# Transposes in place of two POOL reductions, and the feed-forward weights made ready inside the scan stage

## The reference

```python
x = x + _L0_attn_ref(_layernorm(x), context, Wq, Wk, Wv, Wout, bout)
...
x = x + _L1_attn_ref(_layernorm(x), A, W_b, b_b, W_c, b_c, D, W_t, b_t, W_o, b_o)   # decay scan over 64 steps
x = x + _L1_ffn_ref(_layernorm(x), W_fc, b_fc, A_fc, B_fc, W_proj, b_proj, A_proj, B_proj)

def fake_quant_weight(w):
    scale = jnp.max(jnp.abs(w)) / 127
    wq = jnp.clip(jnp.round(w / scale), -128, 127) * scale
    return w + jax.lax.stop_gradient(wq - w)

def qat_lora_linear(x, W, b, A, B):
    return x @ fake_quant_weight(W).T + b + 2.0 * ((x @ A.T) @ B.T)
```

## Time and profile before

| what | us |
|---|---|
| median of 3 runs (lowest, highest) | 3278.88 (3271.15, 3282.62) |
| time of the profiled execution | 3276.0 |
| its span, first to last instruction | 3274.2 |
| TensorE busy | 3023.0 (92% of the span) |
| VectorE, ScalarE, POOL busy | 2199.9, 2009.3, 926.0 |
| mean granted TensorE clock | 0.963 |
| wide prologue: first load issued, first score product | 658.4, 721.1 |
| scan stage: first load issued, last vector pass ends | 2914.6, 3025.0 |
| feed-forward stage: first load issued, `fc` of block 0, `project` of block 0 | 3029.4, 3063.1, 3094.2 |

### The profile page before, as it was taken

How to read it: one execution, slowest core, us unless ns; L and a number is a source line. 1 busy time by engine, 2 the same in 40 slices (tenths; PEclk the granted TensorE clock), 3 DMA queues, 4 the chain that set the end, 5 groups by cost and what they waited for, 6 DMA issues and landing times. The chain is left out here.

```text
span 3274.2 us, 88570 instructions
## 1 busy us (share of the span) xinstructions
PE 3023.0 (92%) x34175; PEld 2461.8 (75%) x34175; DVE 2199.9 (67%) x5201; ACT 2009.3 (61%) x3697; POOL 926.0 (28%) x800
## 2 busy tenths in 40 slices
PE   8999999959999999999977999999999997878699
PEld 6888888737877877877866887787787786544598
DVE  5777777756666666666634778778778776664643
ACT  5777777647767667767733666666666675332353
POOL 3444444336555555655620000000000000110110
PEclk9999999969999999999988999999999999889699
DMA  2112111148887888887973111111111110741200
GB/s 79 58 59 66 62 58 58 38 104 151 150 136 145 150 136 148 152 146 140 173 197 119 34 41 53 47 41 47 54 41 47 47 34 24 230 141 52 88 20 26
DMA packets 664877, 294.34 MB, mean 90 GB/s; under 512 B 550747, under 2 KB 639792, under 8 KB 664576
## 3 DMA queue, kind: packets, MB, share of 16 engines
q1 hardware_dynamic: 626176, 237.71, 34.1%
q10 hardware_dynamic: 38400, 52.44, 4.8%
HBM read 125.95 MB, written 29.88 MB: 48 GB/s over the span
## 5 line engine op out<-in xcount | busy, mean ns | idle before, releaser
L1096 POOL TENSOR_TENSOR wide_parts<-wide_prob,wide_parts 128x1024 f16<-128x1024 f32 x256 | 548.7, 2143 | 398.1 <-ACT wide_parts L1282 329.9
L1385 DVE TENSOR_REDUCE wide_row_max<-wide_score 128x1 f32<-128x1024 f32 x256 | 312.7, 1221 | 163.2 <-PE wide_score L1130 161.6
L1130 PE MATMUL wide_score<-wide_kT,wide_qT 128*128 128x512 f32 x1536 | 413.1, 404 | 7.1 <-ACT wide_prob L1270 5.5
L1270 ACT ACTIVATE wide_prob<-wide_score,wide_neg_max 128x1024 f32<-128x1024 f32 x256 | 285.2, 1114 | 163.7 <-DVE wide_neg_max L1388 158.2
L641 ACT ACTIVATE mask_prob<-mask_prob,mask_row_min 128x256 f32<-128x256 f32 x512 | 232.1, 503 | 161.6 <-DVE mask_row_min L730 161.6
L1130 PEld LDWEIGHTS wide_score<-wide_kT,wide_qT 128*128 128x128 f32 x1536 | 277.1, 189 | 67.9 <-issue 8.9
L1282 ACT ACTIVATE wide_parts<-wide_prob 128x1024 f16<-128x1024 f32 x256 | 269.9, 1054 | 18.5 <-ACT wide_prob L1270 9.2
L2217 DVE TENSOR_REDUCE cell_row_max<-cell_score 128x8 f32<-128x512 f32 x192 | 131.2, 684 | 171.6 <-PE cell_score L1853 169.8
L1146 PE MATMUL wide_turn<-wide_probT,wide_v 128*128 128x256 f16 x1536 | 189.6, 273 | 2.8 <-DMA wide_probT<-wide_parts 2.8
L1146 PE MATMUL wide_pv<-wide_probT,wide_v 128*128 128x256 f16 x1536 | 190.3, 274 | 1.2 <-DMA wide_probT<-wide_parts 1.2
L111 POOL TENSOR_TENSOR cell_var_eps<-cell_mean_var,const_eps 128x4 f32<-128x4 f32 x8 | 1.6, 200 | 670.5 <-DVE cell_mean_var L105 670.5
(11 more groups left out here) (338 smaller groups left out, 6878.3 us busy)
## 6 DMA issues: line engine op xcount, KB each, us to landing
cell_w_stage<-cell_weights ACTq DMA_DIRECT2D x24, 768.0 KB, 6.0
mask_ctx<-in_ctx SPq DMA_DIRECT2D x32, 512.0 KB, 3.9
ctx_ctx<-in_ctx SPq DMA_DIRECT2D x32, 512.0 KB, 4.4
...
wide_probT<-wide_parts SPq DMA_TRANSPOSE x512, 3.3
...
```

The lines of the kernel that those rows point to most:

```text
L1096: pool.tensor_tensor(parts[:, s % 2, LO, :], prob[:, s % 2, :], parts[:, s % 2, HI, :], ALU.subtract).then_inc(part_lo, 1)
L1130: mm = pe.matmul(score[:, s % 2, half * 512:(half + 1) * 512], qT[:, u_par, a, s * P:(s + 1) * P], kT[:, par, b, half * 512:(half + 1) * 5 ...
L1270: act.activation(prob[:, s % 2, :], score[:, s % 2, :], ACT.Exp, bias=neg_max[:, s % 2:s % 2 + 1], scale=SHARP, accum_out=row_sum[:, u_par ...
L1385: dve.tensor_reduce(row_max[:, one], score[:, s % 2, :], AX.X, ALU.max).then_inc(max_found, 1)
```

## The change

Three things. In the wide prologue the two reductions on POOL give way to two small transposes on TensorE with a row maximum and a spreading copy on VectorE between them; all `rstd_of` of POOL then stand in a row ahead of its bias additions, and the load of the whole W_v is issued one place earlier, ahead of block 1. The preparation of the feed-forward weights moves into a class `FfnWeights`, whose loads stand at the end of the scan stage's load queue and whose passes are placed in the scan's steps 1 to 7; its maxima go by transposes too, its low parts are subtracted on POOL, and it uses three PSUM banks (3, 6, 7) by turns. And x stays in SBUF from the scan to the feed-forward stage: the scan no longer stores it and the last stage no longer loads it. The scan's steps are written out instead of looped.

```diff
+    def vector_max(self, dve, m):
+        name = self.NAMES[m]
+        dve.wait_ge(self.w_loaded[name], 16)
+        dve.tensor_reduce(self.amax[:, m:m + 1], self.flat(self.w[name]), AX.X, ALU.max, apply_absolute_value=True).then_inc(self.max_found, 1)
+    def tensor_max_rows(self, pe, bank):
+        pe.wait_ge(self.max_found, 2)
+        pe.transpose(bank[0:2, 0:P], self.amax[:, :], self.ident[:, :]).then_inc(self.max_turned, 1)
+    def vector_spread_max(self, dve, bank):
+        dve.wait_ge(self.max_turned, 1)
+        dve.tensor_reduce(self.all_max[:, :], bank[0:2, 0:P], AX.X, ALU.max).then_inc(self.max_spread, 1)
+        dve.wait_ge(self.max_spread, 1)
+        dve.tensor_scalar(self.max_row[:, :], self.all_max[:, :].to_broadcast([2, P]), 1.0, None, ALU.mult).then_inc(self.max_spread, 1)
+    def tensor_share_max(self, pe, bank):
+        pe.wait_ge(self.max_spread, 2)
+        pe.transpose(bank[:, P:P + 2], self.max_row[:, :], self.ident[0:2, 0:2]).then_inc(self.max_shared, 1)
+    def vector_quantise(self, dve, bank, m):
+        one, steps = slice(m, m + 1), m * 4 + 1
+        src, q = self.flat(self.w[self.NAMES[m]]), self.flat(self.wq[self.NAMES[m]])
+        if m == 0:
+            dve.wait_ge(self.max_shared, 1)
...
+            dve.tensor_scalar(self.scale[:, :], bank[:, P:P + 2], 1.0 / self.QMAX, None, ALU.mult).then_inc(self.quant_step, 1)
+        dve.wait_ge(self.quant_step, 1)
+        dve.reciprocal(self.inv_scale[:, one], self.scale[:, one]).then_inc(self.quant_step, 1)
+        dve.wait_ge(self.quant_step, steps + 1)
+        dve.tensor_scalar(q, src, self.inv_scale[:, one], self.MAGIC, ALU.mult, ALU.add).then_inc(self.quant_step, 1)
...
+        dve.tensor_scalar(q, q, self.QMAX, self.scale[:, one], ALU.min, ALU.mult).then_inc(self.quant_step, 1)
...
+        dve.tensor_tensor(q, q, src, ALU.subtract).then_inc(self.rest_found, 1)
+        dve.wait_ge(self.rest_found, m + 1)
+        dve.tensor_tensor(q, src, q, ALU.add).then_inc(self.quant_done, 1)
...
+    def bank_of(self, pe, banks, kind, n):
+        i = self.uses.index((kind, n))
+        if i >= 3:
+            before, m = self.uses[i - 3]
+            pe.wait_ge(self.prep_copied if before == "turn" else self.weights_ready, m + 1)
+        return banks[i % 3]
+    def tensor_turn(self, pe, banks, first, end):
+        if first == 0:
+            pe.wait_ge(self.small_loaded, self.SMALL_LOADED)
+        elif first == self.small_turns:
+            pe.wait_ge(self.quant_done, 1)
+        elif first == self.fc_turns:
+            pe.wait_ge(self.quant_done, 2)
+        for n in range(first, end):
+            dst, parts = self.turns[n]
+            bank = self.bank_of(pe, banks, "turn", n)
+            at = 0
+            for src, width in parts:
+                k = src.shape[0]
+                mm = pe.transpose(bank[0:src.shape[1], at:at + k], src, self.ident[0:k, 0:k])
+                at += k
+            mm.then_inc(self.prep_turned, 1)
+    def scalar_copy(self, act, banks, first, end):
+        for n in range(first, end):
+            dst = self.turns[n][0]
+            bank = banks[self.uses.index(("turn", n)) % 3]
+            act.wait_ge(self.prep_turned, n + 1)
+            act.activation(dst, bank[0:dst.shape[0], 0:dst.shape[1]], ACT.Copy).then_inc(self.prep_copied, 1)
+    def tensor_low_rank(self, pe, banks, first, end):
+        pe.wait_ge(self.prep_copied, self.fc_turns if first < self.fc_loras else len(self.turns))
+        for n in range(first, end):
+            out, lhsT, rhs, _ = self.products[n]
+            bank = self.bank_of(pe, banks, "lora", n)
+            pe.matmul(bank[:, 0:rhs.shape[1]], lhsT, rhs, start=True, stop=True).then_inc(self.lora_ready, 1)
+    def vector_merge(self, dve, banks, first, end):
+        for n in range(first, end):
+            out = self.products[n][0]
+            bank = banks[self.uses.index(("lora", n)) % 3]
+            dve.wait_ge(self.lora_ready, n + 1)
+            dve.scalar_tensor_tensor(out, bank[:, 0:out.shape[1]], self.LORA, out, ALU.mult, ALU.add).then_inc(self.weights_ready, 1)
+    def scalar_hi(self, act, first, end):
+        for n in range(first, end):
+            out, _, _, split = self.products[n]
+            act.wait_ge(self.weights_ready, n + 1)
+            act.activation(split[self.HI], out, ACT.Copy).then_inc(self.w_hi, 1)
+    def gpsimd_lo(self, pool, first, end):
+        for n in range(first, end):
+            out, _, _, split = self.products[n]
+            pool.wait_ge(self.w_hi, n + 1)
+            pool.tensor_tensor(split[self.LO], out, split[self.HI].bitcast(F32), ALU.subtract).then_inc(self.w_lo, 1)
...
+            if n == 1:
+                sp.dma_start(w_v_all, W_v.rearrange("(t p) i -> p t i", p=CP)).then_inc(w_v_loaded, 16)
             sp.dma_start(x_all[:, n * SUB:(n + 1) * SUB, :], block_rows(x_in[n * BLK:(n + 1) * BLK, :])).then_inc(x_loaded[n], 16)
             if n == 0:
                 weights(0, 0)
                 sp.dma_start(out_bias[:, :], b_out.partition_broadcast(P)).then_inc(bias_loaded, 16)
-            if n == 1:
-                sp.dma_start(w_v_all, W_v.rearrange("(t p) i -> p t i", p=CP)).then_inc(w_v_loaded, 16)
         weights(0, 1)
...
-        for n in range(2):
-            rstd_of(n)
-        for m in range(2):
-            pool.wait_ge(top_found, m + 1)
-            pool.partition_all_reduce(all_top[:, m:m + 1], top[:, m:m + 1], P, RMAX).then_inc(top_shared, 1)
-        for n in range(2, NBLK - 1):
+        for n in range(NBLK):
             rstd_of(n)
         pool.wait_ge(bias_loaded, 16)
-        add_bias(0)
-        rstd_of(NBLK - 1)
-        for n in range(1, POOL_BIASES):
+        for n in range(POOL_BIASES):
...
+            if n == 1:
+                pe.wait_ge(top_found, 2)
+                pe.transpose(misc_ps[0:2, 0:P], top[:, :], ident[:, :]).then_inc(top_turned, 1)
+                pe.wait_ge(top_spread, 2)
+                pe.transpose(misc_ps[:, P:P + 2], top_row[:, :], ident[0:2, 0:2]).then_inc(top_shared, 1)
...
+        def spread_top():
+            dve.wait_ge(top_turned, 1)
+            dve.tensor_reduce(all_top[:, :], misc_ps[0:2, 0:P], AX.X, ALU.max).then_inc(top_spread, 1)
+            dve.wait_ge(top_spread, 1)
+            dve.tensor_scalar(top_row[:, :], all_top[:, :].to_broadcast([2, P]), 1.0, None, ALU.mult).then_inc(top_spread, 1)
         def scale_values():
-            dve.wait_ge(top_shared, 2)
-            dve.tensor_tensor(bound[:, :], all_top[:, 0:1], all_top[:, 1:2], ALU.mult).then_inc(v_scaled, 1)
+            dve.wait_ge(top_shared, 1)
+            dve.tensor_scalar(bound[:, :], misc_ps[:, P:P + 1], CD / V_TOP, None, ALU.mult).then_inc(v_scaled, 1)
             dve.wait_ge(v_scaled, 1)
-            dve.tensor_scalar(v_up[:, :], bound[:, :], CD / V_TOP, 1e-30, ALU.mult, ALU.max).then_inc(v_scaled, 1)
+            dve.tensor_scalar(v_up[:, :], misc_ps[:, P + 1:P + 2], bound[:, :], 1e-30, ALU.mult, ALU.max).then_inc(v_scaled, 1)
             dve.wait_ge(v_scaled, 2)
             dve.reciprocal(v_down[:, :], v_up[:, :]).then_inc(v_scaled, 1)
...
         find_top(1, w_v_all)
+        spread_top()
         stats_of(2)
         scale_values()
...
-    turn_banks, in_banks, out_banks, prep_banks = bank[0:2], bank[2:4], bank[4:6], bank[6:8]
+    turn_banks, in_banks, out_banks, prep_banks = bank[0:2], bank[2:3], bank[4:6], bank[6:8]
+    ffn_banks = [bank[3], bank[6], bank[7]]
...
-        step(0, 0, True)
-        with eng.Fori(0, (NBLK - 4) // 2) as i:
-            for k in (1, 2):
-                step(i * 2 + k, k % 2, False)
-        for n in range(NBLK - 3, NBLK):
-            step(n, n % 2, False)
+        for n in range(NBLK):
+            step(n, n % 2, n == 0)
...
+        ffn.load(sp)
...
-        with pool.Fori(0, NBLK) as n:
+        for n in range(8):
             norm.gpsimd_rstd(pool, n)
+        ffn.gpsimd_lo(pool, 0, ffn.loras)
...
+            if n == 7:
+                ffn.tensor_turn(pe, ffn_banks, ffn.fc_turns, len(ffn.turns))
...
+            if n == 3:
+                ffn.tensor_share_max(pe, ffn_banks[2])
...
+            if n == 2:
+                ffn.tensor_max_rows(pe, ffn_banks[2])
+            if n == 4:
+                pe.wait_ge(ffn.quant_step, 1)
+                ffn.tensor_turn(pe, ffn_banks, 0, ffn.small_turns)
+            if n == 5:
+                ffn.tensor_turn(pe, ffn_banks, ffn.small_turns, ffn.fc_turns)
+            if n == 6:
+                ffn.tensor_low_rank(pe, ffn_banks, 0, ffn.fc_loras)
...
+        ffn.tensor_low_rank(pe, ffn_banks, ffn.fc_loras, ffn.loras)
...
-        def store(n):
-            act.wait_ge(y_ready, (n + 1) * 2)
-            act.dma_start(block_rows(x_out[rows(n * BLK, BLK), :]), of_block(n)).then_inc(y_stored, 16)
...
-            store(n)
+            if n == 4:
+                ffn.scalar_copy(act, ffn_banks, 0, ffn.small_turns)
+            if n == 5:
```

(53 more changed lines are left out.)

281 lines of the change are left out of this document (105 added, 176 removed).

## The result

| | before | after |
|---|---|---|
| median of 4 runs each on one chip, us | 3275.92 | 3246.22 |
| lowest, highest | 3271.15, 3282.62 | 3242.45, 3248.70 |
| time and span of the profiled execution | 3276.0, 3274.2 | 3242.45, 3240.5 |

The ratio is 0.9907 (95% interval 0.9885 to 0.9929): 29.7 us faster by the medians, 33.6 by the profiled executions (the profiled execution of the changed kernel was the fastest of its four). I had said 3245, a gain of 32.4.

A forecast was written before the change was run, and what follows sets the result against it. TensorE's own work was taken to bound the kernel, except at stage starts, where chains between engines do. 9.5 + 23.9 - 1.0 = 32.4 us of gain, forecast as 3245 us, range 3235 to 3258.

The forecast's parts named there:

- Wide prologue, 9.5 us: Start of wide attention: replacing POOL's reductions and their pauses by small transposes brings block 3's normalising 9.5 us earlier.
- no POOL pause over 1 us: Wide prologue: expected sign in the profile that POOL no longer pauses longer than 1 us.
- Scan, 18.2 us later: Scan stage: preparing the feed-forward weights there makes its last work end at 3043.2 instead of 3025.0, 18.2 us later.
- My three additions, 0.4, 2.0 and 2.4 us: Scan steps 2 and 3 together, 4, and 5: TensorE time added by weight transposes, delaying block 6's output by 4.9 us.
- Between the stages, 27.1 us: From the scan's end to block 0's second product in the last stage: 27.1 us, with all weights ready.
- The tail's sum, 23.9 us: Scan's end and last stage: the old 69.2 us less 18.2 and 27.1 leaves a gain of 23.9 us.
- One more clearing, 1.0 us: End of the program: one further clearing costs 1.0 us, taken off the gain.
- 2: Wide prologue: POOL's pauses are not the reductions', so that part gains nothing; 3255 us, chance 0.06.
- 3: Scan step 4 through block 0's first product: clock stays low, costing 47 us; 3292 us, slower, chance 0.03.
- Rival 1: Scan's last steps: TensorE's clock falls, costing 12 to 18 us; 3257 us, chance 0.10.
- The prediction's own sign of being wrong, a clock near 0.5 in the scan's last steps: Scan's last steps: a granted TensorE clock near 0.5 there would show the forecast wrong.
- spread between runs: Whole kernel: 3 us of the range's widening, beside 2 us of prologue either way.

The follow-up runs named there:

- `wide_alone`: The kernel before with only the new wide attention (small transposes for the GpSimd reductions, W_v loaded one place earlier); 3266.57 us, ratio 0.9970 to the kernel before.
- `scan_end`: The changed kernel with W_proj's low-rank products and merges between the halves of block 7's output, not behind both; 3245.09 us, ratio 0.9898 to the kernel before.
- `after_again`: The changed kernel run once more, unaltered, as a yardstick on the same chip; 3245.61 us, ratio 0.9910 to the kernel before.

## Why the prediction was right

- **Wide prologue, 9.5 us.** The mechanism held, the stage's total came partly by luck. From the start of W_v's maximum to block 3's normalising lie 10.27 us (673.55 to 683.82), against 20.10 before: 9.8. From the end of W_v's maximum to the next statistics it took 0.82, where I had 0.9. From the start of that maximum the first score product comes 34.6 us later instead of 44.5, 9.85 us earlier. My sign "no POOL pause over 1 us" was too sharp: there are longer waits, such as the 2.98 us above, all of them for VectorE. What I had left out is what comes after: the first score products now can run before the clock rises. In the trace of after the first twelve took 5.46 us instead of 2.98 (2.98 to 5.46 over the nine traces with the new prologue and no unused transposes), so that from the first turning to the first product with V 7.6 us are left, and 7.0 to 9.9 over the nine, 8.1 on average. The stage as a whole came out at 1009.8 us on average over the nine, against 1019.9: 10 us. Part of the difference is the key products ahead of the change, which took 3.70 us in five of the nine and about 6 in both old ones. In the four traces where they took 5.8 us or more, the stage takes 1011.3 on average: compared like with like the gain is 8.6 us.
- **Scan, 18.2 us later.** The sum held, one term of it did not. At the scan's first turnings the program runs 8.6 us earlier. Against that, block 6's output starts 4.1 us late (I had 4.9), block 7's 12.2 (11.5), and the scan ends 18.8 late. GpSimd's eight low parts took 5.51 us, not 5.9. (My three additions, 0.4, 2.0 and 2.4 us, make 4.8; I wrote 4.9.) The mis-sized term is W_proj's turning: its sixteen transposes took 3.68 us at a granted clock of 0.50, where the sixteen of W_fc a step earlier had taken 1.53 + 0.66. These 1.5 us, and 0.2 more on the first output rows behind (1.37 instead of 1.13), were nearly made up by the shorter steps ahead.
- **Between the stages, 27.1 us.** 26.5, up to `project` at 3061.61. The step from the scan's end (3029.65 + 5.51 = 3035.16) to the first statistics took 0.93 where I had 1.4; the rest stood as worked out, VectorE's wait for GpSimd included. The store and load of x that I subtracted as a whole are 4 us of it.
- **The tail's sum, 23.9 us.** `project` of block 0 starts 23.9 us earlier, counted from the same upstream point. In seven traces with this tail it takes 333.4 to 334.2 us, against 356.6 and 358.4: 23.7 on average. In the first pair of traces 1 us more is won behind that point, since block 0's `project` took 11.45 us instead of 12.45.
- **One more clearing, 1.0 us.** Wrong and small: from the last store's issue to the span's end 4.3 us, and 4.6 before, so it cost nothing.
- **Rivals.** 2 is refuted by `wide_alone`. 3 did not happen. Rival 1 happened for 6.8 us: in all twelve traces with the weights in the scan the granted clock fell to 0.50, 2.0 to 2.9 us after the low-rank products of W_fc began, and it was back ahead of most of block 7's output (0.95 from 3021 to 3028). The prediction's own sign of being wrong, a clock near 0.5 in the scan's last steps, was thus there for part of them, at the cost of the 1.7 us named above and of up to 1 us in the low-rank products themselves (4.90 us, and 3.84 at my price). `scan_end` shows what more of it costs.
- **What no step had.** The unchanged cell stage took 1111.7 and 1112.2 us in the two traces with the old wide stage and 1109.3 to 1118.3, on average 1115.0, in nine with the new one. That accounts for medians of 29.7 to 30.7 us where the two parts gained 34 in their own places (10 and 23.7); my 32.4 lies between, since this loss, which I had not foreseen, outweighs what I had priced too low (the prologue by half a microsecond, the clearing by 1.0). My range covered it as "spread between runs". (2 and 3 us on either side of 3239 and 3255 make 3234 to 3260; I wrote 3235 to 3258.) These 3 us lie in TensorE's pace and not in its waits. The cell stage of the kernel before and of `after_again`, columns as in the earlier trace rows:

```profile
1678.53:2790.25 1111.72, 1019.01 (x17002) 855.50 (x17002) 802.79 (x1408) 687.45 (x1276) 19.32 (x32) 0.97 0.17 55
...
1664.40:2780.52 1116.12, 1023.41 (x17002) 858.01 (x17002) 802.89 (x1408) 688.17 (x1276) 19.37 (x32) 0.97 0.17 55
```

For the same 17002 instructions TensorE is busy 1019.0 and 1019.9 us in the two old traces and 1020.2 to 1025.6, on average 1023.1, in the nine; what is left of the stage is 92.5 and 91.9 us. The time at a granted clock of 0.50 in it goes from 60 and 64 us to between 65 and 78. In the three kernels with unused transposes it is the other way round: the clock is no lower than in those nine (70 to 75 us at 0.50), and 6 to 11 us more lie outside TensorE's busy time. Why the clock is lower for longer, by chance or by the moment at which the stage starts, is open.
